# State space stage: the input product of every group's fourth state made by GpSimd and copied in by ScalarE, gates one step later

## What is computed

```python
xc = _silu(conv(x_in) + conv_b)                      # 256 channels
dt = softplus(einsum('blr,rd->bld', dt_r, W_dt) + b_dt)
A = -exp(A_log)                                      # 256 channels x 16 states
def step(h, inp):
    dt_t, B_t, C_t, u_t = inp
    dA = jnp.exp(dt_t[:, :, None] * A)
    h = h * dA + dt_t[:, :, None] * B_t[:, None, :] * u_t[:, :, None]
    y = jnp.einsum('bdn,bn->bd', h, C_t)
    return (h, y)
_, ys = lax.scan(step, h0, xs)                       # over 128 time steps
y = (ys + xc * D_param) * _silu(z)
out = x + einsum('bld,de->ble', y, W_out)
```

## Time and profile before

| | us |
|---|---|
| median of 3 runs | 1811.33 (1810.22 to 1811.67) |
| profiled execution, its own time | 1810.44 |
| span in its profile | 1808.6 |
| VectorE busy | 1404.6 (78%) |
| TensorE matmuls busy | 1472.3 (81%) |
| ScalarE busy | 873.3 (48%) |
| GpSimd busy | 894.9 (49%) |

### The profile page before, as it was taken

How to read it: one execution, slowest core, us unless ns; L and a number is a source line. 1 busy time by engine, 2 the same in 40 slices (tenths; PEclk the granted TensorE clock), 3 DMA queues, 4 the chain that set the end, 5 groups by cost and what they waited for, 6 DMA issues and landing times. The chain is left out here.

```text
span 1808.6 us, 29636 instructions
## 1 busy us (share of the span) xinstructions
PE 1472.3 (81%) x9959; PEld 990.4 (55%) x9963; DVE 1404.6 (78%) x2910; ACT 873.3 (48%) x1352; POOL 894.9 (49%) x790
## 2 busy tenths in 40 slices
PE   8999997999789996878887987768998821599990
PEld 3555555989556663333333333336777611599990
DVE  6999995979658878989999999957878767544445
ACT  3555553566545545657566656436566510022225
POOL 4555541444400013777897788645353200377653
PEclk8999998999989998989889988989999955699995
DMA  5000000000000003434444444420000050377755
GB/s 153 2 0 0 0 1 22 9 1 2 1 13 0 0 2 105 140 125 147 138 144 134 147 138 150 132 88 9 9 5 5 2 160 0 134 248 237 236 178 144
DMA packets 86430, 142.94 MB, mean 79 GB/s; under 512 B 13258, under 2 KB 39154, under 8 KB 85794
## 3 DMA queue, kind: packets, MB, share of 16 engines
q1 hardware_dynamic: 80898, 131.71, 22.7%
q0 software_dynamic: 4544, 9.32, 1.4%
q10 hardware_dynamic: 864, 0.33, 0.1%
HBM read 129.31 MB, written 12.00 MB: 78 GB/s over the span
## 5 line engine op out<-in xcount | busy, mean ns | idle before, releaser
L1828 PE MATMUL PS<-m_hC,identf 128*128 128x512 f32 x512 | 274.1, 670 | 83.9 <-POOL m_hC L1579 82.9
L1579 POOL TENSOR_TENSOR m_hC<-m_h,m_Cs 128x1024 f32<-128x1024 f32 x128 | 299.6, 2354 | 86.0 <-DVE m_h L1749 69.3
L1749 DVE TENSOR_TENSOR_SCAN m_h<-m_dA,PS 128x512 f32<-128x512 f32 x256 | 297.2, 1203 | 0.0
L1828 PEld LDWEIGHTS PS<-m_hC,identf 128*128 128x128 f32 x512 | 101.4, 210 | 237.6 <-POOL m_hC L1579 132.9
L1693 ACT ACTIVATE m_dA<-m_DT,m_A 128x508 f32<-128x508 f32 x256 | 166.5, 712 | 38.1 <-DVE m_h L1749 26.5
L1743 DVE TENSOR_TENSOR PS<-PS,m_Bs 128x512 f32<-128x512 f32 x256 | 162.9, 683 | 2.8 <-ACT PS L1684 2.8
L2292 PE MATMUL PS<-e_xT,e_WT 128*128 128x128 f32 x1136 | 139.6, 277 | 0.0
L1982 POOL DMA_INDIRECT e_XG<-token_rows,e_ids x71 | 68.8, 969 | 132.4 <-DVE e_ids L2194 111.1
L2292 PEld LDWEIGHTS PS<-e_xT,e_WT 128*128 128x128 f32 x1136 | 133.8, 194 | 0.0
L2043 ACT ACTIVATE e_Sg<-PS 128x512 f32<-128x512 f32 x71 | 42.4, 597 | 188.2 <-PE PS L2292 188.2
L2207 DVE TENSOR_TENSOR e_HT<-PS,e_Sg 128x512 f32<-128x512 f32 x71 | 49.1, 692 | 100.7 <-PE PS L2292 100.7
(11 more groups left out here) (405 smaller groups left out, 3540.3 us busy)
## 6 DMA issues: line engine op xcount, KB each, us to landing
e_WT<-in_w_wgu SPq DMA_DIRECT2D x71, 512.0 KB, 3.7
m_Bs<-state_rows SPq DMA_DIRECT2D x128, 256.0 KB, 3.2
m_Cs<-state_rows SPq DMA_DIRECT2D x128, 256.0 KB, 3.4
token_rows<-X SPq DMA_DIRECT2D x2, 2048.0 KB
e_Y<-expert_rows SPq DMA_DIRECT2D x16, 256.0 KB, 3.8
k_BD<-in_w_bcr SPq DMA_DIRECT2D x1, 2464.0 KB, 8.9
e_w_wd<-in_w_wd SPq DMA_DIRECT2D x1, 2048.0 KB, 8.0
out_dram<-X SPq DMA_DIRECT2D x8, 256.0 KB, 2.4
```

Of the source, the lines that this page charges most:

```text
L1579: nc.gpsimd.tensor_tensor(hC[:, G % NY], hst[:, G % NH], wide(Cs[:, G % RB, :]), ALU.mult).then_inc(s["hC"], 1)
L1749: nc.vector.tensor_tensor_scan(hst[:, G % NH, ch, :], dA[:, G % NA, ch].rearrange("p b l -> p (b l)"), bank(DBU + ch), 0.0, ALU.mult, ALU. ...
L1828: ins = nc.tensor.matmul(bank(YB + ch), c.identf[:, :], hC[:, G % NY, ch, :], start=False, stop=(n == NS - 1))
```

## The change

At n = TURN = 3 of the groups 1 to 7, VectorE no longer makes the two input products. In their place GpSimd makes one product of 1024 columns into a new tile `own` (stage own_product, index g * 16 + 0.5, between its steps n=0 and n=1), and ScalarE copies its two halves into the PSUM banks DBU (stage own_copied, index g * 16 + 4.45, between the exponentials of n=4 and n=5). Each copy waits for GpSimd's product and for the scan of n=2 of its half, which frees the bank. The copies count in dBu as the products did. The product `inputs`, which writes m_DU for the next group, waits for the own product too.

The gate moves from index 17.5 to 18.5 for all groups but the first, where it was 18.5 already. Group 0's output matmuls, statistics and norm move one to two indices later. x2 moves behind step 15 of the group (from -17.5 to -16.45; for group 2 from 13.5 to 15.5, and x3 there from 14.5 to 15.6).

```diff
+    own = sb("own", [P, CH, T])
...
+    TURN = 3
...
-    OWN = {"inner_stats": -25.5, "inner_rstd": -25.4, "inner_norm": -20.5, "xn_T": -22.5, "xn_copy": -18.1, "x0": -20.9, "x1": -19.5, "x2": -17.5, "x3": -16.4,
+    OWN = {"inner_stats": -25.5, "inner_rstd": -25.4, "inner_norm": -20.5, "xn_T": -22.5, "xn_copy": -18.1, "x0": -20.9, "x1": -19.5, "x2": -16.45, "x3": -16.4,
            "silus": -12.6, "dt_b_c": -14.5, "parts": -10.6, "dt0": -12.5, "dt1": -12.4, "dt_bias": -8.6, "exps": -7.5, "logs": -6.5,
            "corrected0": -9.5, "corrected1": -7.9, "softplus": -6.4, "inputs": -4.6, "z0": -9.1, "z1": -8.1, "z_copy0": -5.1, "z_copy1": -4.1,
-           "staged": 1.5, "gate": 17.5, "output0": 21.6, "output1": 22.6, "stats": 25.5, "rstd": 25.6, "norm": 30.5, "silu_z": 16.5}
-    EARLY = {0: {"first_inputs": -1, "gate": 18.5, "z0": -1, "z1": 0.5, "z_copy0": 1.4, "z_copy1": 2.4,
-                 "output0": 20.6, "output1": 21.6, "stats": 23.5, "rstd": 23.6, "norm": 28.5},
+           "staged": 1.5, "gate": 18.5, "output0": 21.6, "output1": 22.6, "stats": 25.5, "rstd": 25.6, "norm": 30.5, "silu_z": 16.5,
+           "own_product": TURN - 2.5, "own_copied": TURN + 1.45}
+    EARLY = {0: {"first_inputs": -1, "z0": -1, "z1": 0.5, "z_copy0": 1.4, "z_copy1": 2.4},
...
-             2: {"inner_stats": 3.5, "inner_rstd": 3.6, "inner_norm": 9.6, "xn_T": 10.5, "xn_copy": 16.4, "x0": 11.5, "x1": 12.5, "x2": 13.5, "x3": 14.5, "silus": 19.4,
+             2: {"inner_stats": 3.5, "inner_rstd": 3.6, "inner_norm": 9.6, "xn_T": 10.5, "xn_copy": 16.4, "x0": 11.5, "x1": 12.5, "x2": 15.5, "x3": 15.6, "silus": 19.4,
...
                 if g > 1:
                     pool.wait_ge(s["dup"], CH * g)
+                    pool.wait_ge(s["own"], g - 1)
...
+            def own_product(g, par):
+                G = g * NS + TURN
+                pool.wait_ge(bs[G % RB], 16 * (G // RB + 1))
+                pool.wait_ge(s["dBu"], CH * (G - NS + 1))
+                pool.wait_ge(s["du"], g)
+                nc.gpsimd.tensor_tensor(own[:, :, :], DU[:, :, :], wide(Bs[:, G % RB, :]), ALU.mult).then_inc(s["own"], 1)
...
+            def own_copied(g, par):
+                act.wait_ge(s["own"], g)
+                for ch in range(CH):
+                    act.wait_ge(s["h"], CH * (g * NS + TURN - 1) + ch + 1)
+                    nc.scalar.copy(bank(DBU + ch), own[:, ch, :]).then_inc(s["dBu"], 1)
...
-                for ch in range(CH):
+                for ch in range(CH) if g == 0 or n != TURN else ():
                     if n == 0:
                         dve.wait_ge(s["dup"], CH * g + ch + 1)
```

More of the change, by code:

```diff
@@ L1416, in state_space @@
     s = c.sems("m_", "A cw wc xp0 z0 mone nm n xnp xnT xpc z zc sz u xd bcp bcs dv ab e w l c1 t dt du dup "
-                     "dA dBu h hC o yacc y1 yp ng nb tw x " + LN_SEMS + " ist imv ilv irs")
+                     "dA dBu h hC o yacc y1 yp ng nb tw x " + LN_SEMS + " own ist imv ilv irs")
     bs = list(c.sems("m_", " ".join(f"bs{i}" for i in range(RB))).values())
@@ L1468, in state_space @@
     STORE = [16] + [g * NS + 11 for g in range(1, NG - 1)]
-    LATER = ("corrected0", "corrected1", "softplus", "inputs", "staged")
+    LATER = ("corrected0", "corrected1", "softplus", "inputs", "staged", "own_product", "own_copied")
     def aux(g, ch):
@@ L1589, in norm @@
                 nc.gpsimd.tensor_tensor(no[:, 1, :], no[:, 0, :], ln["rs"][:, :], ALU.mult).then_inc(s["nb"], 1)
-            stages = {"inner_rstd": inner_norm, "corrected0": corrected(0), "corrected1": corrected(1), "softplus": softplus, "inputs": inputs, "rstd": norm}
+            stages = {"inner_rstd": inner_norm, "corrected0": corrected(0), "corrected1": corrected(1), "softplus": softplus, "inputs": inputs, "own_product": own_product, "rstd": norm}
             setup()
@@ L1701, in _ @@
             stages = {"inner_norm": inner_norm, "xn_copy": normalised, "silus": silus, "parts": parts, "dt_bias": step_sizes, "exps": exps, "logs": logs,
-                      "z_copy0": z_copied(0), "z_copy1": z_copied(1), "staged": staged, "silu_z": last_gates, "norm": norm}
+                      "z_copy0": z_copied(0), "z_copy1": z_copied(1), "staged": staged, "own_copied": own_copied, "silu_z": last_gates, "norm": norm}
             setup()
```

## The result

| | before | changed |
|---|---|---|
| median of 7 runs, us | 1811.33 (1809.78 to 1813.66) | 1815.82 (1813.84 to 1819.73) |
| profiled execution (span) | 1810.44 (1808.6) | 1814.09 (1812.3) |
| stage: from the norm ahead of it (L90) to the last gate | 492.47 | 495.93 |
| VectorE waits ahead of gates | 18.4 | 4.9 |
| VectorE waits for the copies | none | 28.0 |

The account below looks back on a forecast made before the run. It took a loop over TensorE, ScalarE and GpSimd, as long as the group, to bound the kernel. New waits of 26.7 us against 23.9 saved gave +2.8, so 1814.1 us from a median of 1811.33; range 1810.5 to 1819.0.

Parts of the forecast that it names:

- The bound: State-space stage: a loop over TensorE, ScalarE and GpSimd lasts the whole group, 59.9 us; VectorE's 58.4 us only fill it.
- What leaves VectorE: 23.9 us leave VectorE: products 8.3, waits before gates 13.9, and group 0's statistics' wait.
- the statistics' wait of group 0: VectorE's wait of 1.74 us at 793.22 goes when group 0's statistics move two indices later.
- The copies: Before the scan of n=3, ScalarE's first copy reaches VectorE 4.98 us after x3's end, behind the SiLU block.
- The boundaries: Six group boundaries, 0 to 1 through 5 to 6: new waits before the scan of n=3, 26.7 us in all.
- TensorE's clock: Low clock after a gap of some 4 us per group; longer, x3 comes 1.35 us later; bounds 1811.4 to 1816.8.
- The size: Whole kernel: +2.8 us, profiled execution 1810.44 to 1813.2, median 1814.1.
- "same": Whole kernel within 0.2%, 3.6 us, of the kernel before, border at 1815.0; chance 0.46.
- Copy hidden: Rival: copies come before ScalarE's SiLU block or it ends earlier; 10 us less, 1801; chance 0.11.
- Low clock behind the gate: Rival: D matmuls run slow after TensorE waits for the gate, 1.3 us at three boundaries; +3.9, 1818; chance 0.18.
- Port lock: Rival: shared SBUF port pushes each GpSimd own product's 2.35 us into VectorE; 16 us more, about 1830; chance 0.03.
- GpSimd's own product: Between GpSimd's products of n=0 and n=1: 2.35 us, covered by its idle time, so nothing waits for it.

Follow-up runs that it names:

- short_product: Kernel before, with the input product of n=3 in groups 1 to 7 made on 8 of 512 columns: 1807.77 us, ratio 0.9978.
- silu_late: Changed kernel with GpSimd's own product earlier, copies behind the exponentials of n=3, SiLU block behind those of n=4: 1805.02 us, 0.9964 of the kernel before.
- short_loop: Changed kernel without own product and copies, SiLU block behind the exponentials of n=4, softplus before those of n=8: 1801.13 us, 0.9947 of the kernel before.
- own_only: Changed kernel with gate, x2 and group 0's stages at their old places, own product and copies kept: 1815.36 us, 1.0020 of the kernel before.
- turn5: Changed kernel with the product of n=5 given to GpSimd instead of n=3's, copies at 5.35: 1805.27 us, 0.9971 of the kernel before.
- gpsimd_only: Kernel before, plus an unread GpSimd product of 1024 columns in groups 1 to 7, no copies: 1811.92 us, ratio 1.0004.
- copy_first: Changed kernel with the copies moved ahead of ScalarE's SiLU block (index n=3 + 0.35 instead of + 1.45): 1805.86 us, 0.9968 of the kernel before.
- short_loop_own: silu_late with the next group's softplus right behind dt_bias, before the exponentials of n=8 and n=9: 1798.40 us, 0.9926 of the kernel before.

## Why the prediction was right
**The bound** held to 0.3 us a group, but I had drawn the loop wrongly. I called it one over TensorE, ScalarE and GpSimd that VectorE only fills, 59.4 us long without it. In the kernel before it runs through VectorE too, from the gate to the scan of n=3: 4.24 us from x3's end to that scan, 6.80 to the step sizes, 48.91 to the next x3's end, 59.95 in all. What saved the reading is that TensorE's own order is nearly as long, 59.7 (short_product, silu_late). So VectorE's 1.05 us less in short_product gave 0.3 a group, and in silu_late, with no copy waited for, the 1.2 us of the own product gave nothing until the last group. In short_loop the groups shortened with the loop, to 58.41 us, where a loop over softplus and the exponentials of n=8 holds them.

**What leaves VectorE** was right in kind: the gate waits went to 4.9 us, the statistics' wait of group 0 is gone, L1759 has 14 instructions less and the same length (680 ns). (One count is off and enters no sum: between 941.38 and 953.50 lie seven steps and projections of 1.72 us, not six.)

**The copies** were right to the hundredth: the scan starts 4.98 us after x3's end in the first boundary (770.86 to 775.84) and at 954.59 to 959.57, and in the other four within 0.01 of it. GpSimd's product and VectorE's instructions kept their lengths. This is the term that the result rests on. The balance of 26.7 us of new waits against 23.9 us saved is right as bookkeeping, but it isn't what sets the time: own_only saves almost nothing ahead of the gates and ends at the same stage length, because the loop of x3, copies, scan and step sizes takes the same time in both.

**The boundaries,** waits before the scan of n=3 in us:

| groups | 0 to 1 | 1 to 2 | 2 to 3 | 3 to 4 | 4 to 5 | 5 to 6 | sum |
|---|---|---|---|---|---|---|---|
| forecast | 6.6 | 2.6 | 5.8 | 3.2 | 4.0 | 4.5 | 26.7 |
| measured | 7.0 | 3.8 | 3.9 | 4.6 | 4.4 | 4.3 | 28.0 |

The sum is nearer than its parts, which miss by up to 1.9 us either way; that is luck. The middle ones miss mostly by the term that I had bounded and not forecast, TensorE's clock. In group 2, where the kernel before had its long form, the changed one had none:

```profile
873.72 1.99 PE L1844 MATMUL PS<-m_hC,identf 128*128 128x512 f32 x4 [3.77 <-POOL m_hC L1582]
876.03 1.98 PE L1844 MATMUL PS<-m_hC,identf 128*128 128x512 f32 x4 [0.33 <-POOL m_hC L1582]
```

This is the same pair of steps as in the earlier trace rows, after nearly the same gap (3.77 and 3.61 us), at full clock. In groups 3 and 4 the changed kernel had the long form (6.38 and 6.31 us for two steps) where I had counted a short one (5.18 and 5.40 before). In group 1 two steps took 5.40 us right ahead of the projections, where before the low clock had passed by then, and x3 came 1.2 us later than forecast.

The path was partly another one as well. At groups 2 to 3 I had the step sizes held by the scan of n=3, and TensorE's order held them; at groups 3 to 4 I had them held by the D matmuls behind the gate, and the scan held them, as at the two boundaries after. Counted from the norm they start at 213.2 us against 213.6 forecast, and at 274.8 against 274.7. The two paths end within 0.7 us of each other, so the mix-up cost little. The hops themselves were a little short: 6.80 us where I had 6.6, 10.7 where I had 10.5.

**The size.** Of the profiled execution I forecast 1813.2 and it took 1814.1: +3.7 instead of +2.8. The stage gave 0.7 of the difference: counted from the norm, the last x3 ended at 386.0 us against 385.3, with the long clock form in three groups of four where I had kept two. On the medians the change is +4.5, or 0.25%, inside the range but past the border of 0.2% that I had set for "same". So the class that I had held likeliest, "same" at 0.46, did not come, and slower, at 0.43, did, though the interval of 0.15 to 0.34% leaves either open. My chance for "same" stood on a forecast only 0.9 us under that border. The rest of the 4.5, about 1 us, no profile of mine places.

**The rivals.** Copy hidden did not happen; what it would have given, I had put at 10 us, and silu_late and turn5 show 6.5 (0.36%) and 5.3 us. Low clock behind the gate: the D matmuls waited for the gate in five boundaries, 0.3 to 1.1 us, and took 1.98 us, not 3.18; only in group 7, after 5.27 us, they took 3.40. My gap of 2.4 us at groups 1 to 2 was 1.1, since x3 came later. Port lock: gpsimd_only rules it out for these forms. The Trainium skill says of offloading between GpSimd and VectorE that it "might not help", because they share a read port ("Perfetto Trace Analysis", "Optimizing Scalar/DVE Operations"). It did not help here, but not by the port: seven more products on GpSimd left VectorE's scans at 1201 ns (1203 before) and the whole at 1.0004.

**Wrong in my reading:** that GpSimd's own product is always early enough. It is, where the copies come late anyway; in copy_first it was the last to come. And the price of the own product where nothing waits, 1.2 and not 2 to 3 us.

## What to carry to other kernels
Before a bottleneck engine is relieved, follow the chain around it for a whole period: if a loop over the other engines is as long as its busy time, less work on it turns into a wait, and only the last pass gains. Look too at which stretch of the bottleneck engine's own work lies on the loop: in short_product and in short_loop_own that decided what a microsecond less was worth. A hand-over through an in-order engine costs what stands ahead of it in that engine's stream, and what that in turn waits for, not its own length; moving one index here was worth 8 us of the stage (copy_first), the work handed over 1.2 (silu_late). Gains of separate parts don't add when they end in the same wait: time each part alone.

## What the runs showed of the hardware
TensorE after a gap of 3.5 to 4.2 us in each group: mostly it goes on at its lower clock (1.2 GHz) for a part or most of two steps (5.1 to 6.8 us for the two, 3.6 at full clock), sometimes at the higher (2.4 GHz), in the same kernel and after gaps of the same length. Stretches of the changed kernel (us, busy PE, granted clock, DMA share, GB/s), groups 2 and 3:

```profile
873.00:880.00 7.00, 5.69 (x12) 1.00 0.51 150
...
934.00:941.00 7.00, 6.37 (x9) 0.57 0.51 150
```

The gaps ahead of them were 3.77 and 3.76 us. A long form instead of a short one moves the next x3 by 0.7 to 1.3 us (48.9 to 49.1 us from the step sizes to x3's end, or 49.7 to 50.2). It may be part of why runs of one kernel spread over 4 to 6 us; that was not tested.
